# Layer 0 attention: the value product of a head group as one run of 64 matmuls instead of four runs of 16

## What is computed

```python
h = jnp.maximum(_layernorm(x), 0.0)
Q, K, V = proj(Wq, bq), proj(Wk, bk), proj(Wv, bv)      # (b, 8 heads, 1024, 32)
scores = jnp.einsum('bhnd,bhmd->bhnm', Q, K) * SCALE
scores = jnp.where(adj[:, None] == 0, -jnp.inf, scores)
attn = jax.nn.softmax(scores, axis=-1)
out = jnp.einsum('bhnm,bhmd->bhnd', attn, V)
x = x + out.transpose(0, 2, 1, 3).reshape(b, n, 256) @ Wo.T + bo
```

## Time and profile before

| What | us |
|---|---|
| median of three runs | 3978.39 |
| the three runs | 3978.39, 3991.85, 3978.27 |
| span of the profiled execution, first to last instruction | 3976.3 |
| TensorE matmuls busy in it | 3669.7 (92%) |
| VectorE busy | 3128.6 (79%) |
| ScalarE busy | 2267.1 (57%) |
| GpSimd busy | 674.9 (17%) |
| scores, L837, 2048 matmuls | 754.4 |
| transposes, L856, 8192 | 1098.6 |
| value product, L873, 16384 | 649.7 |

### The profile page before, as it was taken

One profiled execution on the slowest core, in us unless ns is written; L12 is line 12 of the kernel. 1 busy time (PEld: TensorE's weight loads), 2 busy tenths in 40 slices (PEclk: granted clock), 3 DMA queues, 4 the chain that ended last, 5 costly groups with the idle time before them and its releaser, 6 DMA issues.

```text
span 3976.3 us, 94630 instructions
## 1 busy us (share of the span) xinstructions
PE 3669.7 (92%) x34096; PEld 2908.9 (73%) x34096; DVE 3128.6 (79%) x5926; ACT 2267.1 (57%) x3940; POOL 674.9 (17%) x440
## 2 busy tenths in 40 slices
PE   6989989899998989989899898998989989899998
PEld 5777777777777767777777777776777767777776
DVE  6968778687886978869788696886968869688785
ACT  3837547275573845738456384663836638366482
POOL 1021030310303103031020301203012030120300
PEclk8999999999999999999999999999999999999999
DMA  5041220403204032040310503104031040311300
GB/s 151 2 105 36 60 82 2 117 25 70 71 2 118 23 76 66 2 131 10 81 61 4 137 2 83 59 15 126 2 89 53 21 121 2 95 47 31 99 2 12
DMA packets 129070, 227.67 MB, mean 57 GB/s; under 512 B 20672, under 2 KB 71104, under 8 KB 128448
## 3 DMA queue, kind: packets, MB, share of 16 engines
q1 hardware_dynamic: 128448, 219.50, 20.3%
HBM read 101.98 MB, written 16.78 MB: 30 GB/s over the span
## 4 chain that ended last, share of the span: by engine, by line
PE 68%; SPq 11%; issue 9%; DVE 7%; DMA 2%; ACT 1%; DVEq 0%; POOL 0%; POOLq 0%; ACTq 0%
PE pT L856 21%; PE ps L837 15%; PE pO L873 13%; SPq L220 11%; PE ps L773 8%; PE pO L975 7%; PE pT L908 2%; DMA adj_half<-in_adj_dram 2%; PE pT L963 2%; DVE pt L525 1%; DVE most L483 1%; DVE sm L667 1%; PE pO L884 1%; DVE sm L510 1%; DVE sm L674 1%
## 5 line engine op out<-in xcount | busy, mean ns | idle before, releaser
L349 ACT ACTIVATE sm<-sm,mn 128x1024 f32<-128x1024 f32 x1024 | 1179.5, 1152 | 454.8 <-DVE mn L510 452.5
L510 DVE CUSTOM_DVE_ANT_0 sm<-ps,bias 128x1024 f32<-128x1024 f32 x1024 | 1250.9, 1223 | 197.5 <-PE ps L837 178.0
L856 PE MATMUL pT<-ident,sm 128*128 128x128 f32 x8192 | 1098.6, 276 | 40.3 <-DVE pt L525 37.1
L856 PEld LDWEIGHTS pT<-ident,sm 128*128 128x128 f32 x8192 | 961.3, 142 | 218.5 <-DVE pt L525 52.8
L837 PE MATMUL ps<-ks,qs 96*128 96x512 f32 x2048 | 754.4, 451 | 4.6 <-issue 3.7
L525 DVE COPY pt<-pT 128x512 f32<-128x512 f32 x1024 | 702.4, 686 | 31.5 <-PE pT L856 30.8
L873 PE MATMUL pO<-pt,v 128*32 128x128 f32 x16384 | 649.7, 278 | 4.8 <-DVE pt L525 4.8
L359 ACT COPY pt<-pT 128x512 f32<-128x512 f32 x1024 | 583.2, 570 | 56.7 <-PE pT L856 56.4
L290 POOL TENSOR_SCALAR bias<-adj_half 128x512 bf16<-128x512 int32 x240 | 468.0, 1950 | 864.3 <-DMA adj_half<-in_adj_dram 855.7
L873 PEld LDWEIGHTS pO<-pt,v 128*32 128x32 f32 x16384 | 388.2, 109 | 170.1 <-issue 170.1
L975 PE MATMUL pO<-h,pt 128*128 128x256 f32 x2048 | 463.0, 379 | 0.0
(11 more groups left out here) (104 smaller groups left out, 3526.5 us busy)
## 6 DMA issues: line engine op xcount, KB each, us to landing
adj_half<-in_adj_dram SPq DMA_DIRECT2D x256, 256.0 KB, 2.8
ks<-pt SPq DMA_DIRECT2D x384, 128.0 KB, 2.4
qs<-pt SPq DMA_DIRECT2D x384, 128.0 KB, 2.4
xf<-in_x_dram SPq DMA_DIRECT2D x16, 1024.0 KB, 8.0
x<-in_x_dram SPq DMA_DIRECT2D x16, 1024.0 KB, 5.7
out_dram<-x SPq DMA_DIRECT2D x128, 128.0 KB, 2.9
x<-in_L_gnn_Wq_dram SPq DMA_DIRECT2D x1, 256.0 KB, 2.8
x<-in_L_gnn_Wk_dram SPq DMA_DIRECT2D x1, 256.0 KB, 3.1
```

What stands on the lines that cost most here:

```text
L349: nc.scalar.activation(sm[:, t % RING, :], sm[:, t % RING, :], ACT.Exp, scale=-1.0, bias=mn[:, t:t + 1], accum_out=den[:, t:t + 1]).then_i ...
L510: nc.vector.tensor_tensor_reduce(out=sm[:, t % RING, :], in0=ps[t % 2][:, :], in1=bias[:, node, :], scale=1.0, scalar=3e38, op0=ALU.add, o ...
L856: last = nc.tensor.transpose(pT[c][:, j * P:(j + 1) * P], sm[:, t % RING, m * P:(m + 1) * P], ident[:, :])
```

## The change

The helper `values` loses its argument `part` and issues all 64 matmuls of a group with its waits in front. It is called once in a group instead of four times: in the second tile of the next group (t % 4 = 1), after the scores of t + 2 and before the transposes of t. Before, quarters ran behind the transposes of the tiles 0, 1, 2 and 3 of the next group.

```diff
-                def values(g, part):
+                def values(g):
                     hg, quad = g // NT, g // 4
-                    if part == 0:
-                        pe.wait_ge(pt_made[0], TILES * b + HG * (g + 1))
-                        pe.wait_ge(pt_made[1], TILES * b + HG * (g + 1))
-                    if g % 4 == 0 and quad and part == 0:
+                    pe.wait_ge(pt_made[0], TILES * b + HG * (g + 1))
+                    pe.wait_ge(pt_made[1], TILES * b + HG * (g + 1))
+                    if g % 4 == 0 and quad:
                         pe.wait_ge(r_copied, QUADS * b + quad)
                         pe.wait_ge(normed, QUADS * b + quad - 1)
                     n = slice(g % 4 * P, (g % 4 + 1) * P)
-                    for m in range(NT // 4 * part, NT // 4 * (part + 1)):
+                    for m in range(NT):
...
-                    if part == 3:
-                        last.then_inc(av, 1)
+                    last.then_inc(av, 1)
...
                 for t in range(TILES):
                     if t + 2 < TILES:
                         scores(b, t + 2)
+                    if t > HG and t % HG == 1:
+                        values(t // HG - 1)
                     transposes(t)
-                    if t >= HG:
-                        values(t // HG - 1, t % HG)
                     if t and t % 16 == 0:
                         rows(t // 16 - 1)
-                for part in range(4):
-                    values(GROUPS - 1, part)
+                values(GROUPS - 1)
                 rows(QUADS - 1)
```

## The result

| | before | after |
|---|---|---|
| median, us (4 runs each) | 3980.89 | 4025.67 |
| range of the runs | 3978.27 to 3991.85 | 4021.58 to 4031.67 |
| span of the profiled execution | 3976.3 | 4022.7 |
| matmuls busy in it | 3669.7 (92%) | 3619.3 (90%) |
| VectorE busy | 3128.6 (79%) | 3098.0 (77%) |

The ratio is 1.0116, with a 95% interval of 1.0093 to 1.0140: the change makes the kernel slower by 1.2%. The forecast was slower by 0.6% (4002 us). The direction and the mechanism were right; the size was half of what came, 23.6 us of 46.4 in the spans. The median lies inside the stated range.

The account below looks back on a forecast made before the run. TensorE bound the kernel before; after, a loop of waits through VectorE holds groups at 8.30 us. With uncovered extras and the layer's end, +1.57 a graph, 15 x 1.57 = 23.6, gives 4002 us; range 3960 to 4045.

Parts of the forecast that it names:

- TensorE saves over 1 us a group: TensorE's work for a group of four tiles: 7.39 us after the change, 8.62 before, from fewer array switches.
- scores to value strips: TensorE's change from score matmuls to the value run: taken as 0.32 us, least 0.23, most 0.23 + 0.20.
- Rival 3: On TensorE, the change from scores to value matmuls costs a full switch, 0.43 us: 26 us more, 4028; chance 0.20.
- The loop through VectorE: Waits from pT transposes through scores, value run, VectorE's masks and copies: a group can't come faster than 8.30 us.
- Rival 1: TensorE remains the bound at 7.39 us a group, 14.8 us less a graph, 3741 us in all; chance 0.03.
- The extras: VectorE's work between masks and copies, per graph: row factors 2.64 us, statistics 1.26, aggregation 1.04, no longer covered by TensorE.
- Rival 2: Groups stay at 8.30 us, but row factors, statistics and aggregation find cover: 54 us less, 3924 us; chance 0.12.
- 0.33 to the last transpose: TensorE, second half of the transposes of tile 4k, first to last: 0.33 us of the 8.30 a group.
- 0.62 to its mask: From the second score matmul of tile 4k + 4 to VectorE's mask: 0.62 us of the 8.30 a group.
- The last three tiles: End of layer 0, to the last value run: 7.13 us before, 7.72 after, +0.59 a graph.
- The last graph: The graph without statistics or aggregation: its extra time was taken as 0, leaving 15 graphs at +1.57 us.
- rival 4: TensorE's new waits drop the granted clock to half level once a graph: at most 27 us in all, 4029; chance 0.03.

## Why the prediction was right in direction and short in size

- **TensorE saves over 1 us a group: right.** The one price that no row showed, scores to value strips, was taken as 0.32 and is 0.32. Rival 3, with a full switch there, is out. The reason given for 0.32 (0.09 more for a switch) fits the one number and was not tested further.
- **The loop through VectorE takes it back: right.** Plain groups were forecast at 8.30 and are 8.36 or 8.44. Rival 1 (7.39) is out, by the added instructions above all. The Trainium skill's page TensorEngine Tiling (Array Packing), section Key Properties, has the drain at a change of tiling mode; the trace agrees in so far as each switch has a price (0.20 for 0.11 between transposes and value matmuls, 0.32 for 0.23 behind scores). With two runs the saved switches pay; with one the saving doesn't reach the end.
- **The extras lie on the loop: right.** Row factors 0.88, as forecast; statistics and aggregation 2.13 a graph where 2.30 were forecast (0.33, 0.50 and 1.31 over the plain groups beside them, for tiles 20 to 24, 24 to 28 and 28 to 32). Rival 2 is out.
- **The step that failed is the size of the loop's own terms.** (a) "0.33 to the last transpose": a half that comes out of a wait takes 0.38 from first to last (median of 392 halves in the trace after, for 0.33 in the 434 that didn't wait). The earlier trace rows had it: the waiting half is 0.66 long beside 0.62 for the other, and I used such a 0.39 for the row transposes and not here. 14 x 0.05 x 15 = 10.5 us. (b) "0.62 to its mask": where the node block changes in the first half of the layer, the mask has another wait in front, for the mask bias (`mask_made`, which my description of the kernel leaves out), and the lag is 0.71 (before too, where TensorE's work covered it). I took the lag from tile 62, in the second half. It is on the loop six times, at the tiles 8 to 28: 6 x 0.09 x 15 = 8 us; at tile 28 a statistics instruction stands in front as well, and the run with the early wait took 6 us off in the trace. (c) The last three tiles take 7.91 instead of 7.72, 3 us. (d) The last graph, put at 0, costs 0.9. The statistics and the aggregation cost 2.13 a graph and not 2.30, 2.5 us less, half of it where they overlap with the wait of (b) at tile 28. In sum 20 of the 21.4 us between 23.6 and 45.0.
- Together: from tile 4 to tile 60, second half to second half, before 120.17 and after 122.32, +2.15 for the forecast +0.98; then to the last run 7.12 and 7.91, +0.79 for +0.59. 15 x 2.94 + 0.9 = 45.0 of the 46.4 us that the spans differ by. The remaining 1.4 lies between the layers, whose times scatter by more than that.
- **The clock (rival 4): out for the change.** Its mean over the run is 0.968 after and 0.967 before, and the stage is at 1.00 in all sixteen graphs, as in this stretch (us, then PE, PEld, DVE, ACT and POOL busy, PEclk, DMA share, GB/s):

```profile
571.90:702.50 130.60, 123.37 (x1568) 92.21 (x1570) 112.87 (x205) 103.08 (x181) 8.63 (x11) 1.00 0.01 2
```

## What to carry to other kernels

An engine that shows as 99% busy may be one loop of waits away from another bound. Before merging work on it, follow one period from a waiting instruction back to itself, with the other engines' fixed orders and buffer counts, and sum the starts: here that gave the sign, the place where extras hurt, and a better version. Take each term from a place that waits as the loop will wait, and from each kind of tile: two terms read from other places are most of what the forecast missed. Long runs pay only as far as the neighbour's backlog bridges them: with two score buffers and one transpose buffer that was half a group, 32 matmuls, not 64.

## What was not expected

How much more place counts than work: one run of 64, moved from in front of eight transposes to behind them, costs another 2.4% (1.0359 against 1.0116), and 240 statistics instructions of 0.42 us cost 71 us or none by their place in a group of four tiles. A wait that is always met already still takes 0.09 us in front of the mask (0.71 against 0.62): the last mask bias of the graph shown was written by 559.4 us, before tile 4, and the lag at tile 16 is 0.71 all the same, until the wait is moved (0.63). And remedies that seemed to overlap in the medians add to within 0.1 us in the trace, once the stretch between the layers, where the clock differs from one execution to the next, is left out.
